# Two lists of expert tiles instead of one, own places for the last two batches, and the gates of a batch turned by one transpose

## The reference

```python
xn = layernorm(x)
x = x + cosformer(xn) + soft_moe(xn)     # linear attention, 16 heads; 2 shared experts + top 4 of 16, 64 wide
xn = layernorm(x)
x = x + rope_attention(xn) + top1_moe(xn)  # causal softmax attention, 16 heads of 8; 8 experts, 512 wide
```

## Time and profile before

| | |
|---|---|
| time, median of 3 runs | 1231.99 us (1230.94 to 1232.93) |
| the profiled execution, its own time | 1232.06 us |
| its span, first to last instruction | 1230.7 us |
| PE busy | 1154.9 us (94%) |
| ACT, DVE, POOL busy | 906.8, 902.7, 637.2 us |
| mean granted TensorE clock | 0.975 |

### The profile page before, as it was taken

The page is one execution under the profiler, slowest core; times in us unless marked ns, Lnnn a source line. Parts: engine busy times, 40 slices in busy tenths (PEclk is TensorE's granted clock), DMA queues, the critical chain, the costliest instruction groups (busy, mean ns, idle before and its releaser), DMA issues.

```text
span 1230.7 us, 28493 instructions
## 1 busy us (share of the span) xinstructions
PE 1154.9 (94%) x9792; PEld 685.6 (56%) x9792; DVE 902.7 (73%) x2439; ACT 906.8 (74%) x1224; POOL 637.2 (52%) x857
## 2 busy tenths in 40 slices
PE   6778999999999999999999999999997889899998
PEld 3344454545454545455554545454543466799997
DVE  4548888888888888888888888888879573345554
ACT  3133887878787888788888878787884868567775
POOL 2342646474646565555646464746463202048886
PEclk9778999999999999999999999999997899999999
DMA  4760607152433526160606061424464400025543
GB/s 142 176 132 14 129 16 165 41 106 68 79 99 48 116 38 121 27 135 12 137 10 137 21 127 43 104 70 76 104 180 83 124 23 10 19 43 63 62 58 31
DMA packets 93802, 98.11 MB, mean 80 GB/s; under 512 B 12624, under 2 KB 73552, under 8 KB 93264
## 3 DMA queue, kind: packets, MB, share of 16 engines
q1 hardware_dynamic: 80960, 86.72, 32.3%
q0 software_dynamic: 12272, 8.92, 5.6%
q10 hardware_dynamic: 432, 0.66, 0.1%
HBM read 68.98 MB, written 26.23 MB: 77 GB/s over the span
## 4 chain that ended last, share of the span: by engine, by line
PE 74%; ACT 12%; DVE 7%; issue 5%; POOL 2%; DMA 0%; ACTq 0%; DVEq 0%; POOLq 0%
PE PS L803 11%; PE PS L688 11%; PE PS L843 10%; PE PS L638 7%; PE PS L770 6%; PE PS L788 5%; PE PS L854 5%; ACT flow L957 4%; ACT L957 3%; PE PS L630 3%; PE PS L652 2%; DVE nm L1226 2%; PE PS L755 2%; PE PS L619 2%; ACT early L881 2%
## 5 line engine op out<-in xcount | busy, mean ns | idle before, releaser
L1398 POOL TENSOR_SCALAR_AFFINE_SELECT flow<-flow 128x256 f32<-128x256 f32 (+1 forms) x448 | 192.1, 442 | 343.2 <-ACT flow L957 340.6
L957 ACT ACTIVATE flow<-PS 128x1024 f32<-128x1024 f32 x320 | 319.6, 1027 | 42.8 <-PE PS L788 41.6
L1226 DVE TENSOR_REDUCE nm<-PS 128x2 f32<-128x1024 f32 x128 | 154.8, 1221 | 64.4 <-PE PS L755 64.3
L948 ACT COPY qp<-PS 4x1024 f16<-4x1024 f16 x128 | 128.2, 1002 | 64.7 <-PE PS L778 63.6
L803 PE MATMUL PS<-flow 128*32 128x512 f32 (+3 forms) x2048 | 169.0, 449 | 2.0 <-POOL flow L1398 0.5
L688 PE MATMUL PS<-early,down 128*128 128x512 f32 x288 | 148.9, 629 | 9.1 <-POOL early L1383 9.1
L1383 POOL TENSOR_TENSOR early<-early 128x512 f32<-128x512 f32 x120 | 152.5, 1293 | 8.4 <-DMA early<-gate_rows 8.1
L638 PE MATMUL PS<-xnT,up 128*128 128x512 f32 x288 | 147.0, 613 | 0.0
L1422 POOL DMA_INDIRECT out_y<-X,rowu x71 | 110.5, 1556 | 60.5 <-DMA out_y<-X 34.0
L843 PE MATMUL PS<-xsT,w1s 128*128 128x128 f32 x1136 | 139.2, 276 | 1.2 <-DVE act L1325 1.1
L1322 DVE SCALAR_TENSOR_TENSOR tanh<-tanh,PS 128x512 f32<-128x512 f32 x71 | 48.8, 687 | 121.0 <-ACT tanh L991 105.0
(11 more groups left out here) (164 smaller groups left out, 1998.8 us busy)
## 6 DMA issues: line engine op xcount, KB each, us to landing
early<-gate_rows SPq DMA_DIRECT2D x128, 256.0 KB, 4.7
qp<-relay_q SPq DMA_DIRECT2D x64, 128.0 KB
kp<-relay_k SPq DMA_DIRECT2D x64, 128.0 KB
xsb<-xs SPq DMA_DIRECT2D x71, 65.0 KB, 1.9
relay_k<-qkh SPq DMA_DIRECT2D x32, 128.0 KB, 6.5
out_y<-X SPq DMA_DIRECT2D x16, 256.0 KB, 6.8
early<-in_w SPq DMA_DIRECT2D x1, 4096.0 KB, 12.6
relay_q<-qkh SPq DMA_DIRECT2D x16, 128.0 KB, 2.3
```

Of the source, the lines that this page charges most:

```text
L948: ins = act.copy(m.qp[b % 2][at:at + MR, 2 * g:2 * g + 2, :], rows)
L957: act.activation(m.pt[:, n % RING, :], m.PS[:, i:i + 2, :].rearrange("p k c -> p (k c)"), ACT.Exp, scale=1.0 / SCALE).then_inc(s["exp"], 1)
L1226: dve.tensor_reduce(nm[:, 3, 2 * n:2 * n + 2], ps, AX_X, ALU.max, negate=True).then_inc(s["max"], 1)
L1398: ins = pool.affine_select(part, part, [[0, part.shape[1]], [1, P]], ALU.is_ge, nothing, base=0, channel_multiplier=-1)
```

## The change

There are four edits.

**One transpose for the gates.** PE turns all four token tiles at once, 128 x 64 into 64 x 128, where it had four transposes of 128 x 16 into 16 x 128. ACT copies 64 x 128 instead of 16 x 512, and the write to DRAM has 64 rows of 128 instead of 16 of 512. `gate_rows` holds the same, and its reads are unchanged.

**Two lists.** The first list is computed after batch 12 is ranked. It names only tiles that are full by then, and of it the first 24 (`EARLY`) are used. `taken` keeps how many of them each expert has given, and the second list, after batch 15, continues from there. Tiles 0 to 23 wait for nothing of the last three batches, apart from memory: the first `load` and the first `staged` wait for `y_mm` of batch 15, the transpose in its stage `x1`. `pads` moves behind the load of tile 22.

**Places.** Batches 14 and 15 get tables of their own, and `LAST` is new.

**Memory.** Tensors that must live longer (`jc`, `rowu`, `xsT` and others) move out of the region that is reused.

```diff
+EARLY = 24
 LAST = placed(
-    w1=[-30.389],
-    w2=[-4.773],
-    tables=[-17.626, -12.442, -9.988],
-    listed=[-8.078],
-    pads=[-13.818],
+    w1=[-26.791],
+    w2=[-8.539],
+    tables=[-72.699, -69.568, -68.658, -9.458, -8.659, -3.598],
+    listed=[-63.726, -3.483],
+    pads=[13.86],
...
-NBETWEEN = 22
+NBETWEEN = 25
...
-OWN = {0: AT_B0, 1: AT_B1, 2: AT_B2}
+OWN = {0: AT_B0, 1: AT_B1, 2: AT_B2, B - 1: AT_E1, B - 2: AT_E2}
...
+def ranked(order):
+
+    return sum(name == "ranks" for name, _, _ in order[:order.index(("tables", 0, 0))])
...
     def gT(b, i):
         pe.wait_ge(s["gate"], b + 1)
         ps = bank(("gT", b, i))
-        for t in range(NT):
-            ins = pe.transpose(ps[0:NR0, t * P:(t + 1) * P], m.gate[:, t, :], ident)
-        ins.then_inc(s["gT_mm"], 1)
+        pe.transpose(ps[0:NT * NR0, 0:P], m.gate.rearrange("p t r -> p (t r)"), ident).then_inc(s["gT_mm"], 1)
...
-        act.copy(m.gT, wk(("gT", b, i))[0:NR0, :]).then_inc(s["gT"], 1)
+        act.copy(m.gT, wk(("gT", b, i))[0:NT * NR0, 0:P]).then_inc(s["gT"], 1)
...
-        sp.dma_start(m.gate_d, m.gT).then_inc(s["d_gate"], 16)
+        sp.dma_start(m.gate_d.rearrange("r (t l) -> t r l", t=NT), m.gT).then_inc(s["d_gate"], 16)
...
     def staged(_, n):
         if n == 0:
             act.wait_ge(s["tables"], 1)
+            act.wait_ge(s["y_mm"], B)
             act.wait_ge(s["d_w1"], 16)
+        if n == EARLY:
+            act.wait_ge(s["tables"], 2)
...
     def outputs(_, n):
         act.wait_ge(s["yo_mm"], n + 1)
         if n == 0:
+            act.wait_ge(s["d_out"], 16 * ahead)
+        if n == NT * ahead:
             act.wait_ge(s["d_out"], 16 * (B - 2))
...
     def scatter(_, n):
         if n == 0:
+            pool.wait_ge(s["d_out"], 16 * ahead)
+        if n == EARLY:
             pool.wait_ge(s["d_out"], 16 * (B - 2))
             pool.wait_ge(s["d_last"], 16 * 2)
             pool.wait_ge(s["d_spare"], 16)
...
-        sp.wait_ge(s["d_sorted"], 16 * NT * B)
+        sp.wait_ge(s["rotated"], 2 * B)
         sp.dma_start(m.w2[:, :], io["w2"]).then_inc(s["d_w2"], 16)
...
     def load(_, n):
         u = n % U
         if n == 0:
+            sp.wait_ge(s["y_mm"], B)
+            sp.wait_ge(s["d_sorted"], 16 * NT * ahead)
+            sp.wait_ge(s["tables"], 1)
+        if n == EARLY:
             sp.wait_ge(s["d_pad"], 32 * (E1 + 1))
             sp.wait_ge(s["d_sorted"], 16 * NT * B)
-            sp.wait_ge(s["tables"], 1)
+            sp.wait_ge(s["tables"], 2)
```

More of the change, by code:

```diff
@@ L352 @@
     store=[26.41])
-OWN = {0: AT_B0, 1: AT_B1, 2: AT_B2}
+AT_E1 = placed(
+    stats0=[-58.229],
+    norm0=[-48.083],
+    xnT0=[-47.659],
+    kvr=[-46.563, -45.697, -45.656, -43.784],
+    up=[-42.37, -41.167, -38.968, -38.939, -38.43, -37.953, -36.031, -35.189, -34.34],
+    q=[-41.872],
+    kv=[-41.308],
+    route0=[-43.296],
+    gate=[-41.1],
+    attn0=[-40.164],
+    gT=[-40.114],
+    at0T=[-39.455],
+    down=[-36.147, -36.088, -34.996, -33.175, -32.082, -31.834, -29.18, -28.916, -28.732],
+    gated=[-39.866, -39.405, -37.969, -37.667, -36.134, -35.936, -32.907, -30.355],
+    x1=[-27.637],
+    stats1=[-27.337],
+    norm1=[-26.144],
+    xnT1=[-25.181],
+    rope=[-24.315, -23.747],
+    parts=[-23.903, -20.942],
+    relay=[-18.072],
+    v=[-18.211],
+    logits=[-20.374],
+    route1=[-20.002],
+    expert=[-19.311],
+    ranks=[-18.006],
+    sort=[-19.551, -15.392, -15.382, -10.061],
+    score=[0.372, 1.479, 2.081, 5.302, 5.684, 7.058, 7.725, 8.139, 11.572, 12.322, 12.798, 14.176, 14.275, 14.503,
+           15.275, 15.584, 16.33, 16.497, 17.858, 19.115],
+    max=[-8.411, -7.633, -7.002, -4.311, -2.864, -2.785, -0.416, -0.119, 1.79, 2.038, 2.853, 3.898, 5.122, 5.216,
+         5.392, 6.749, 7.755, 8.508, 9.57, 9.739],
+    mparts=[-2.846, 2.257, 6.154, 10.14],
+    mrows=[-1.413, 5.25, 11.442, 12.01],
+    value=[3.061, 11.15, 12.913, 14.122, 15.737, 17.061, 18.675, 19.875],
+    sums=[14.323, 21.043],
+    heads=[17.893, 23.092],
+    mT=[24.494],
+    out=[25.425],
+    store=[32.375])
@@ new lines @@
+AT_E2 = placed(
+    stats0=[-58.463],
+    norm0=[-48.064],
+    xnT0=[-47.393],
+    kvr=[-46.232, -45.699, -44.756, -44.034],
+    up=[-42.912, -40.571, -38.734, -38.643, -38.476, -37.593, -36.379, -35.999, -34.972],
+    q=[-41.948],
+    kv=[-40.855],
+    route0=[-42.489],
+    gate=[-40.504],
+    attn0=[-39.789],
+    gT=[-39.701],
+    at0T=[-37.776],
+    down=[-34.97, -34.291, -33.254, -31.768, -31.74, -29.218, -28.926, -28.728, -28.689],
+    gated=[-38.22, -37.777, -35.968, -35.792, -35.079, -34.162, -32.095, -29.871],
+    x1=[-27.771],
+    stats1=[-26.691],
+    norm1=[-26.387],
+    xnT1=[-25.643],
+    rope=[-24.781, -23.203],
+    parts=[-23.953, -19.926],
+    relay=[-19.367],
+    v=[-18.678],
+    logits=[-24.544],
+    route1=[-23.229],
+    expert=[-18.541],
+    ranks=[-18.03],
+    sort=[-18.823, -17.247, -16.924, -9.61],
+    score=[-0.171, 0.258, 0.626, 1.216, 2.646, 5.65, 5.757, 7.249, 11.561, 12.304, 12.591, 13.114, 13.399, 13.853,
+           14.243, 14.584, 16.371, 16.488, 16.754, 18.467],
+    max=[-8.293, -8.002, -7.229, -5.329, -4.264, -2.202, -2.154, -1.581, -1.003, 0.208, 1.986, 3.461, 5.205, 5.299,
+         5.3, 5.695, 6.878, 7.298, 8.52, 9.762],
+    mparts=[-4.116, 1.975, 7.405, 10.185],
+    mrows=[-2.42, 5.171, 10.822, 11.726],
+    value=[2.962, 11.374, 12.357, 12.971, 15.909, 16.167, 18.629, 18.886],
+    sums=[13.03, 19.217],
+    heads=[14.448, 22.209],
+    mT=[22.81],
+    out=[24.244],
+    store=[26.411])
@@ L484, in place @@
     m.begins = sb("begins", [P, E1 + 2])
+    m.below = sb("below", [P, E1 + 1, E1])
+    m.mine = sb("mine", [P, 3, E1 + 1])
+    m.taken = sb("taken", [P, E1 + 1])
+    m.lead = sb("lead", [P, E1 + 1])
     m.jr = sb("jr", [P, 4])
+    m.jc = sb("jc", [P, P])
+    m.rowu = sb("rowu", [P, NTILE], U32)
+    m.xsT = sb("xsT", [P, 2, P])
     m.ji = sb("ji", [P, 3, NTAB], I32)
@@ L827, in listed @@
     def listed(b, i):
[L828 removed]
+        pe.wait_ge(s["columns"], i + 1)
         pe.transpose(bank(("listed", b, i))[:, 0:P], m.jc[:, :], ident).then_inc(s["listed_mm"], 1)
@@ L868, in scalar_program @@
     act = nc.scalar
+    ahead = ranked(order)
     def wk(stage, n=0):
@@ L1015, in vector_program @@
     dve = nc.vector
+    ahead = ranked(order)
+    assert EARLY <= NT * ahead - (E1 - 1)
     chain = [0]
```

88 lines of the change are left out of this document (50 added, 38 removed), and 59 rows, old and new, of tables (hidden, load, outputs, rows).

## The result

The changed kernel took **1235.74 us** (median of 7 runs, 1234.34 to 1239.03), the kernel before in the same rounds 1230.94 us (1228.41 to 1232.93). The ratio is 1.0042, with a 95% interval of 1.003 to 1.0054: slower by 4.8 us, where 14.35 us less were forecast. The profiled execution has a span of 1234.4 us, against 1230.7.

The account below looks back on a forecast made before the run. PE was taken as the bound in the full stretch and the last 135 us, with gaps from 905 to 1085. 7.1 − 0.65 + 6.4 + 1.5 = 14.35 us off 1232.06 gave 1217.7 us, range 1205 to 1228.

Parts of the forecast that it names:

- The gates: Gate transposes: three of four leave PE's program, 6.1 us in batches 2 to 15, 1.0 in 0 and 1; 7.1 gained.
- nothing, were a new wait to fill the place: Lower bound for the gate transposes in batches 2 to 15: no gain, against 8.1 us as upper bound.
- rival 4: No change, 1232 us: later DRAM write of 64 gate rows makes `down` wait, tiles give nothing; chance 0.05.
- The first list: Batch 13's first layer: 22 small chained DVE operations, bounds 0 and 4.4 us, plus one PE transpose; 0.65 us lost.
- The places of batches 14 and 15: Stretch 925 to 957: list piece leaves, maxima and ranking change order; 1.5 of 17.1 us lost regained, bounds 0 and 8.5.
- The early tiles: Tail: 7.4 us of tile work moves before batch 15's `out` into PE's gaps; 6.4 us gained, bounds 0 and 19.7.
- rival 1: 977 to 1085: early tiles push attention back by what they take, only gates and list stay; 1225.6 us, chance 0.18.
- near 957: Predicted sign: the first tile's `hidden` starts at batch 15's first maxima, near 957 us, instead of at 975.03.
- Rival 3: 977 to 1065: new gaps bring the mean clock to 0.73, 28.8 us more; 1246.5 us, chance 0.05.

Follow-up runs that it names:

- Experiment 13: Kernel before with each of the gates' four transposes done twice, eight in all: 1234.48 us, ratio 1.0026; a batch takes 58.26 us.
- experiment 1: Kernel before with only the new single gate transpose, and copy and DMA to match: 1231.01 us, ratio 1.0002.
- experiment 2: Changed kernel with the four gate transposes back: 1236.97 us, ratio 1.0041 to the kernel before.
- experiment 6: experiment 5 plus one unit's value matmuls right behind the gates' transpose in the middle batches: 1241.85 us, ratio 1.0093 to the kernel before.
- experiment 11: Changed kernel, list as in experiment 5, batches 14 and 15's first layers at middle places, third up-matmul group behind the middle batches' gate transpose: 1271.67 us, ratio 1.0334.
- experiment 14: experiment 10 plus, in middle batches, the second up-matmul group and its ACT copy moved behind two units with exponentials: 1243.95 us, ratio 1.0105 to the kernel before.
- experiment 4: Changed kernel with the first list's first piece 3.1 us later: 1233.2 us, ratio 1.0018 to the kernel before.
- experiment 5: Changed kernel with the first list's three pieces in the same DVE gap of three batches: 1231.28 us, ratio 0.9993 to the kernel before.
- experiment 10: Changed kernel, list pieces in DVE's gap of three batches, one batch earlier than experiment 5; batches 14 and 15's first layers at middle places: 1227.36 us, ratio 0.9969.
- experiment 7: Kernel before plus four chained DVE operations and two memsets, results unused, where the changed kernel has the list's first piece: 1235.99 us, ratio 1.0037.
- experiment 12: Kernel before with only the own places of batches 14 and 15 added, its list and tail order kept: 1276.53 us, ratio 1.0373.
- experiment 3: Changed kernel without the own places of batches 14 and 15, at the middle batches' places instead: 1285.86 us, ratio 1.0444 to the kernel before.

## Why the prediction was wrong

**The gates: +7.1 forecast, nothing measured.** The step that failed is "There PE is the bound, and whatever leaves its program is gained." I read the chain at the group that opens a batch and took the stretch between two of them as PE's, from the sum of 57.49 of 58.04 us busy. The chain itself says otherwise. In the kernel before, right around the transposes of the earlier trace rows, it reads:

```profile
872.33 0.88 PE PS L638 x2
...
873.84 1.28 ACT L957
...
875.14 1.03 ACT flow L957
...
876.23 0.64 POOL flow L1398
...
876.92 1.55 PE PS L803 x24
...
878.97 1.03 ACT flow L957
880.00 0.54 ACT flow L935 x2
...
880.56 1.28 ACT L881
...
881.86 0.91 ACT early L881 x2
...
883.45 1.28 ACT L957
...
884.74 1.03 ACT flow L957
```

From 873.23 to 885.91 the chain runs through ACT's table loads and exponentials, with one detour over POOL and PE. The transposes at 875.73 are not in it, and the middle batches' chains run the same way: in the whole chain the gates' transposes are a piece only once, in batch 1. PE is busy nearly throughout that stretch, and off the path all the same. Experiment 13 measures the shadow's room (0.23 us on top of the four transposes), and experiments 1 and 2 the value of emptying it (none). The size was off too. I took the 0.58 us from the transposes' start to the next unit's as their work, and it holds a small wait: three fewer shorten their row by 0.33 us (0.60 to 0.27), not by 0.43. The bound "nothing, were a new wait to fill the place" was in the text, and had only the 0.05 of rival 4. Experiments 6, 11 and 14 tried to use the freed time and all lengthened the batch, 11 and 14 with two more table loads of ACT in it; which order of ACT and PE would turn it into a gain stays open.

**The first list: −0.65 forecast, −6.0 measured.** The step was "a batch in which it has 9.0 to spare", with a bound of 4.4, the operations' own step times. In the changed kernel, DVE's shift, POOL's pair of multiplications and the unit of PE that waits read:

```profile
782.93 3.61 DVE L1388 TENSOR_SCALAR ti<-ti 128x8 int32<-128x8 int32 x1
784.02 2.50 POOL L1499 TENSOR_TENSOR early<-early 128x512 f32<-128x512 f32 x2
...
788.37 0.39 PE L862 MATMUL PS<-kp,qp 36*128 36x256 f16 x4 [3.28 <-DVE nm L1329]
```

The step failed twice. DVE's spare time is not where the pieces stand: the one gap of 2.17 us holds one piece, elsewhere the maxima behind a piece are late for PE (experiments 4, 5 and 10). And the price of one operation is not its step time wherever POOL is at work: 3.61 us for the shift of 8 columns in the changed kernel (782.93, 0.17 in the earlier trace rows), 3.47 us for a cast in experiment 7, whose piece alone costs 4.6 us of the period. DVE's busy time in the list's period rose by 7.8 us (49.04 to 56.82), 3.4 of it this one operation, so the bound of 4.4 was wrong. It took the duration from a place where POOL ran only an indirect DMA (939.42 to 940.51), with no multiplications behind it.

**The places of batches 14 and 15: +1.5 forecast.** I priced them only in the tail and counted nothing for their first layers. Those cost 1.0 + 2.8 + 2.5 = 6.3 us (experiment 12); in the changed kernel 2.79 and 2.50 of them show by themselves. The 1.0 can't be found in the list's period, which is as long without the own places (64.28 us in experiment 3). What they bring along is six more table loads on ACT.

**The early tiles: +6.4 forecast.** Here the prediction was right in size. With the 1.5 of the places it gave 7.9 us for the tail, and the tail behind x1 is 7.51 us shorter. Over the five traces with the changed kernel's tail and places it is 307.6 to 310.9 us long, against 315.8 to 316.4 in the four with the tail and places of the kernel before. The two terms can't be measured apart: tail order without places is 365.4 us long, places without tail order 347.8, neither 316.4, both 308.9.

The way was another, and that the sum came so near is luck. `out` came at 1082.64, 163.2 us behind x1, where it was 166.2, with 7.4 us more of tiles ahead of it. Some 10 us of gaps were filled there, not 7.9, and rival 1 did not happen. But behind `out`, where those 7.4 us are missing, only 4.5 are gained: 3.0 us are idle after 1085, where the forecast saw no change. The first `hidden` came at 964.68, which is 45.2 us behind x1, where "near 957" meant 48.4. And the 17.1 us lost in 925 to 957, of which the forecast left all but 1.5 as they were, are 10.8 in the stretch that corresponds to it (4.0 idle, 0.21 × 32 = 6.7 for the clock). Of the 7.51 us, 5.65 are idle time and 1.86 are the same matmuls at a higher clock. A share 1 − clock of a window, as the prediction counted it, is too high a price for the clock, since it charges PE's idle time as well.

**Rivals.** Rival 3 (a lower clock) did not happen: the clock is 1.00 from 977 on. Rival 4 came nearest, by the gates' part, and for another reason: ACT, not the write to DRAM. The outcome, slower by 4.8 us (3.7 in the two traces), is the tail's 7.5 against 6.0 for the list and 5.3 for the first layers, and no rival of mine had these two.

## What to carry to other kernels

An engine that is busy 99% of a stretch need not be its bound. Follow the chain through the very instructions that an edit removes: if they are not pieces of it, removing them can be worth nothing, as here, and doubling them shows how much room there is. A small operation on a nearly full engine is priced by what stands behind it and by what the neighbour engine does at that moment, so look for the gap in its timeline, and put it there. Of a hand-made order, the parts that fit each other have to be found out: the own places of the last batches could not be taken out whole (50 us), but those of the first layer could, and gave 3.6 us back. And what such places cost in the stretch that was full has to be counted too.

## What the runs showed of the hardware

Small DVE operations with SBUF on both sides were held up beside some work of POOL, not by a share but entirely: 3.47 and 3.61 us in place of 0.17, both ending within 0.03 us of POOL's pair of multiplications. A two-input operation of 8 columns took 0.83 us in experiment 4 beside another such pair, and ended within 0.04 us of it. DVE's maxima of 768 and 1024 columns, which read from PSUM, kept their 0.92 to 1.23 us throughout. The Trainium skill, "SBUF — State Buffer", section "Who interferes with whom", says that casts and `tensor_scalar` in their two-port modes, and `tensor_tensor` with two SBUF inputs beside a GpSimd operation that reads SBUF, contend for the port pair that VectorE shares with GpSimd, that this is an exclusive lock and the loser blocks for the whole instruction, while `tensor_reduce` never contends. The trace agrees in kind with each of these; in which mode an operation ran it does not show.

Two things go beyond that. The hold lasted longer than one instruction of POOL: the cast of experiment 7 began during the indirect DMA and outlasted it, the select behind it and the first of the two multiplications. And not all of POOL's work holds such an operation up. The two operations just ahead of that cast took 0.20 and 0.17 us beside the same indirect DMA, and in the kernel before three of them, the two of the earlier trace rows and the cast at 939.87, took 0.17 us each beside another one (939.42 to 940.51). Which of POOL's instructions begins such a hold is not shown.

ACT's table loads took 1.28 us each, and three of them are pieces of the 12.7 us of chain between 873.23 and 885.91, 3.84 us. Two more of them in each batch went with 1.3 us more in experiment 14 and 2.25 in experiment 11, and six more in the last batches with the 6.3 us of experiment 12. So they are a likelier thing to attack in a batch than PE's transposes; no run here has fewer than the kernel before's six in a batch.
